# Softmax denominators in four column groups, one addition per quad, and unread products in every step

## What is computed

```
hi = x[src] @ w1
hj = x[tgt] @ w2
e = leaky_relu(hi + hj, negative_slope=0.3) * a
logits = e.reshape(-1, 8, 16).sum(axis=-1)            # 8 heads
exp = exp(logits - segment_max(logits, tgt)[tgt])
attn = exp / segment_sum(exp, tgt)[tgt]
out = segment_sum(hi.reshape(-1, 8, 16) * attn[:, :, None], tgt)
x = layernorm(x + out)
```

## Time and profile before

| | us |
|---|---|
| median of 3 runs | 2206.56 |
| lowest and highest run | 2199.6 and 2210.35 |
| the profiled execution, its own time | 2204.6 |
| its span in the trace | 2202.5 |

### The profile page before, as it was taken

One profiled execution on the slowest core, in us unless ns is written; L12 is line 12 of the kernel. 1 busy time (PEld: TensorE's weight loads), 2 busy tenths in 40 slices (PEclk: granted clock), 3 DMA queues, 4 the chain that ended last, 5 costly groups with the idle time before them and its releaser, 6 DMA issues.

```text
span 2202.5 us, 47203 instructions
## 1 busy us (share of the span) xinstructions
PE 1800.7 (82%) x12728; PEld 1400.5 (64%) x12729; DVE 1327.6 (60%) x3726; ACT 658.6 (30%) x1410; POOL 1605.9 (73%) x1701
## 2 busy tenths in 40 slices
PE   6678777988788788788969878888888888888886
PEld 6456555666566566566757666666766676666665
DVE  6455665666656666566645456666566566665665
ACT  6111211211111111111114434444444344434442
POOL 5777777777777777777627777777777777777774
PEclk8798998889988998889889999999999999999897
DMA  8722332323323333233255444444444444444441
GB/s 220 159 85 78 89 96 83 96 85 96 95 84 95 96 88 96 85 96 97 60 142 154 138 126 141 127 140 129 141 126 140 129 141 127 132 137 139 129 126 42
DMA packets 239386, 252.31 MB, mean 115 GB/s; under 512 B 141011, under 2 KB 187720, under 8 KB 239315
## 3 DMA queue, kind: packets, MB, share of 16 engines
q1 hardware_dynamic: 185036, 141.15, 21.5%
q0 software_dynamic: 54000, 110.28, 18.0%
q10 hardware_dynamic: 288, 0.13, 0.0%
HBM read 233.20 MB, written 13.22 MB: 112 GB/s over the span
## 4 chain that ended last, share of the span: by engine, by line
POOL 48%; issue 21%; PE 14%; DVE 7%; DMA 4%; DVEq 2%; POOLq 1%; ACT 1%; SPq 0%; ACTq 0%
POOL T L742 27%; POOL G L708 20%; PE ps L1847 2%; PE ps L1824 2%; DMA G<-hi_rows,idx 2%; PE ps L1819 2%; PE ps L1851 1%; DMA T<-y_rows,idx 1%; PE ps L1780 1%; PE ps L2061 1%; PE ps L2052 1%; DVEq L1309 1%; DVE msg L1329 1%; PE ps L2067 1%; PE ps L2073 1%
## 5 line engine op out<-in xcount | busy, mean ns | idle before, releaser
L742 POOL DMA_INDIRECT T<-y_rows,idx x831 | 789.0, 950 | 303.7 <-issue 249.2
L708 POOL DMA_INDIRECT G<-hi_rows,idx x831 | 801.9, 965 | 267.8 <-issue 249.0
L2052 PE MATMUL ps<-G 128*128 128x64 f32 x1664 | 228.5, 284 | 126.8 <-DVE acc L1606 126.2
L2052 PEld LDWEIGHTS ps<-G 128*128 128x128 f32 x1664 | 217.0, 204 | 138.7 <-issue 137.4
L993 ACT ACTIVATE G<-G 128x512 f32<-128x512 f32 x208 | 131.1, 630 | 576.6 <-DVE G L1612 576.6
L1819 PE MATMUL ps<-ident,G 128*128 128x128 f32 x828 | 151.0, 312 | 174.9 <-issue 60.0
L2061 PE MATMUL ps<-wN,G 128*128 128x128 f32 x1664 | 255.7, 302 | 26.3 <-DVE T L1571 26.0
L1612 DVE TENSOR_TENSOR G<-ps,T 128x512 f32<-128x512 f32 x208 | 143.6, 691 | 217.0 <-DMA T<-y_rows,idx 202.3
L890 ACT ACTIVATE V<-ps 128x512 f32<-128x512 f32 x207 | 123.6, 597 | 474.3 <-PE ps L1824 472.3
L1300 DVE TENSOR_TENSOR V<-ps,V 128x512 f32<-128x512 f32 x207 | 141.9, 686 | 179.5 <-ACT V L890 175.5
L2073 PEld LDWEIGHTS ps<-msg,wE 128*128 128x128 f32 x832 | 168.5, 203 | 125.2 <-issue 111.0
(11 more groups left out here) (233 smaller groups left out, 2252.3 us busy)
## 6 DMA issues: line engine op xcount, KB each, us to landing
T<-in_edge_weight SPq DMA_DIRECT2D x103, 512.0 KB
Dbc<-block_destinations SPq DMA_DIRECT2D x69, 384.0 KB
T<-in_edge_attr SPq DMA_DIRECT2D x103, 256.0 KB
G<-hi_rows,idx POOLq DMA_INDIRECT x831
T<-y_rows,idx POOLq DMA_INDIRECT x831, 2.5
link<-scan_destinations SPq DMA_DIRECT2D x280, 16.1 KB
hi_rows<-T SPq DMA_DIRECT2D x12, 256.0 KB, 2.8
mX<-in_x SPq DMA_DIRECT2D x15, 192.0 KB
```

The source lines that it names most:

```text
L708: pool.indirect_dma_start(out=G[:, s, t * C:(t + 1) * C], out_offset=None, in_=hi_d[:, :], in_offset=bass.IndirectOffsetOnAxis(ap=idx[:, s ...
L742: pool.indirect_dma_start(out=Yb[:, r, t * C:(t + 1) * C], out_offset=None, in_=y_d[:, :], in_offset=bass.IndirectOffsetOnAxis(ap=idx[:, r ...
L2052: ins = pe.matmul(aggP[:, 0:W], hS[i][:, n * C:(n + 1) * C], ohB[i][:, n * W:(n + 1) * W], start=(n == 0), stop=(n == 3))
```

## The change

1. `EXs` gets 32 columns per tile (9 used, the rest set to zero once). Each of a quad's four denominator products writes its own group of 32 output partitions, without accumulation across the four. The same in `sum_up`.
2. DVE adds both halves in one instruction per quad, [128, 2, 64]. Half 1 of the accumulator therefore has 128 live partitions, four partial sums of the denominators.
3. Where nodes are read back, PE no longer turns 9 partitions but multiplies the 128 partitions by `gather4`, a [128, 9] matrix with four ones per column that adds the four partial sums; `mD` has 128 partitions.
4. The DMA that clears half 1 covers 128 partitions.
5. `unread`: two products of `ident` with `W12` (256 columns) at the head of each step into `U[0]`, behind the wait for the previous maximum, and two ahead of a step's first aggregate into `AG[0]`.

```diff
-        EXs = sb("EXs", [P, GT, DC])
+        EXs = sb("EXs", [P, GT, 32])
+        gather4 = sb("gather4", [P, DC])
-        mD = sb("mD", [DC, MB * P])
+        mD = sb("mD", [P, MB * P])
+        accD4 = acc[:, 1, :]
...
-                        sp.dma_start(acc[0:DC, 1, :], acc[0:DC, 0, :]).then_inc(s_zero, 16)
+                        sp.dma_start(acc[:, 1, :], acc[:, 0, :]).then_inc(s_zero, 16)
...
-                        act.activation(mD[:, :], accD[:, cut], ACT.Copy).then_inc(s_n["copy"], 1)
+                        act.activation(mD[:, :], accD4[:, cut], ACT.Copy).then_inc(s_n["copy"], 1)
...
+            dve.memset(EXs[:, :, DC:32], 0.0)
+            dve.tensor_reduce(gather4[:, :], ident[:, :].rearrange("p (k h) -> p h k", k=4)[:, 0:DC, :], AX.X, ALU.add)
...
-                        w_ = acc[:, 0, bass.ds(base, W)]
-                        dve.tensor_tensor(w_, AG[j % 2][:, 0:W], w_, ALU.add).then_inc(s_acc, 1)
-                        w_ = accD[:, bass.ds(base, W)]
-                        dve.tensor_tensor(w_, AG[j % 2][0:DC, W:2 * W], w_, ALU.add).then_inc(s_acc, 1)
+                        w_ = acc[:, :, bass.ds(base, W)]
+                        dve.tensor_tensor(w_, AG[j % 2][:, 0:2 * W].rearrange("p (k n) -> p k n", k=2), w_, ALU.add
+                                          ).then_inc(s_acc, 2)
...
+                dve.memset(exsO[:, :, DC:32], 0.0)
                 dve.memset(exsO[:, :, 0:1], 1.0).then_inc(s_n["one"], 1)
...
+                    def unread(n, bank):
+                        for i in range(n):
+                            pe.matmul(bank[:, 0:2 * C], ident[:, :], W12[:, :], start=True, stop=True)
...
                         if j == 0:
+                            need(pe, s_acc, 2 * p * GQ)
+                            unread(2, AG[0])
                             pe.wait_ge(s_oh, p + 1)
...
-                            ins = pe.matmul(AG[j % 2][0:DC, W:2 * W], EXs[:, t, :],
-                                            oh[:, t * W:(t + 1) * W], start=(i == 0), stop=(i == 3))
+                            ins = pe.matmul(AG[j % 2][32 * i:32 * i + 32, W:2 * W], EXs[:, t, :],
+                                            oh[:, t * W:(t + 1) * W], start=True, stop=True, skip_group_check=True)
...
+                    if nq:
+                        need(pe, s_lk, (f - 1) * GQ + 1)
+                        unread(2, U[0])
                     sums(0, b, bs, 2)
...
-                            ins = pe.transpose(AG[1][:, MB * C + i * DC:MB * C + (i + 1) * DC], mD[:, i * P:(i + 1) * P],
-                                               ident[0:DC, 0:DC])
+                            ins = pe.matmul(AG[1][:, MB * C + i * DC:MB * C + (i + 1) * DC], mD[:, i * P:(i + 1) * P],
+                                            gather4[:, :], start=True, stop=True, skip_group_check=True)
```

More of the change, by code:

```diff
@@ L768, in build @@
         atP, h1P, efP, zP, aggP, oP = ps[0], ps[1:3], ps[3:5], ps[5:7], ps[7], ps[5]
-        exsO = R1[:, 0:4 * DC].rearrange("p (t h) -> p t h", h=DC)
+        exsO = R1[:, :].rearrange("p (t h) -> p t h", h=32)
         ohO = ohT[:, 1, :].bitcast(F32)
@@ L1923, in sum_up @@
                         t = 4 * j + i
-                        ins = pe.matmul(AG[j % 2][0:DC, W:2 * W], ex[:, t, :], hot[:, t * W:(t + 1) * W],
-                                        start=(i == 0), stop=(i == 3))
+                        ins = pe.matmul(AG[j % 2][32 * i:32 * i + 32, W:2 * W], ex[:, t, :], hot[:, t * W:(t + 1) * W],
+                                        start=True, stop=True, skip_group_check=True)
                     ins.then_inc(s_agg, 1)
@@ L1995, in _ @@
                     pe.transpose(ps[0][:, i * C:(i + 1) * C], accH[:, n0:n0 + P], ident[:, :])
-                    ins = pe.transpose(ps[3][:, i * DC:(i + 1) * DC], accD[:, n0:n0 + P], ident[0:DC, 0:DC])
+                    ins = pe.matmul(ps[3][:, i * DC:(i + 1) * DC], accD4[:, n0:n0 + P], gather4[:, :], start=True, stop=True,
+                                    skip_group_check=True)
                 ins.then_inc(s_n["t"], 1)
```

## The result

| | us |
|---|---|
| before, median (19 runs) | 2205.89 |
| changed, median (19 runs) | 2212.51 |
| ratio | 1.0027, 95% interval 1.0019 to 1.0035 |
| span of the profiled execution, before and after | 2202.5 and 2208.8 |

The kernel became 6.6 us slower. I had said 2221, so the sign is right and the size is less than half of what I forecast. A trace is that of one execution; its time can lie some us off the median of its kernel.

A forecast was written before the change was run, and what follows sets the result against it. POOL's gathers were taken to pace the softmax part, with no slack before the first reuse of a G slot. Copy 15, head products 1.6 and end -1.0 gave +15.6 us, so 2221 us, range 2208 to 2236.

The forecast's parts named there:

- The place: First reuse of a G slot: POOL waits for messages, and whatever delays the Dbc load's landing delays everything behind.
- The landing below 92 us: Sign at the Dbc load of group 2: expected to land about 98 us; below 92, the copy was over-priced.
- The term of 15 us: Clearing copy ahead of the Dbc load on SP's queue: 3.05 MB more, costing 15 us, with ends 12.3 and 19.8.
- no row here reaches that rate: Clearing copy: no shown row reaches the skill's 436 GB/s, by which the added delay would be 7 us, not 15.
- cheap copy: Rival at the clearing copy: it costs 6.1 us, result about 2212, or 2206 if wholly hidden; chance 0.18.
- Head products, +1.6 us: Two unread products on PE at the head of step 2, ahead of the messages, add 1.6 us to the chain.
- All other steps, 0: Remaining softmax steps: PE gains +0.9 us net per step, hidden by 2.6 us of room, so 0 us.
- the granted clock should stay up: PE through the softmax steps: less idle waiting keeps its clock up; the time saved is spent waiting, 0 us.
- fewer stretched gathers: Rival at POOL's gathers: L1379 never meets a gather's start, giving back 17.4 us, about 2203; chance 0.06.
- Small costs: Per quad of a step: one merged DVE addition takes 290 ns, the denominator sums on PE 0.27 us.
- The end, -1.0 us: From the last gather to the stored y rows: cheaper sums and additions less added products, -1.0 us (-1 to +1).
- the likeliest case: Whole kernel, forecast as priced: 2209 to 2232 us, from the copy's ends, gathers 5 us and runs 4 us either way; chance 0.64.

The follow-up runs named there:

- e1b: The changed kernel with the copy that clears accumulator half 1 issued behind the loads of group 2: 2205.06 us, ratio 0.9994 to the kernel before.
- e2b: The kernel before with only the clearing copy enlarged from 9 to 128 partitions, in its old place: 2211.99 us, ratio 1.0024.
- e11: The changed kernel with half of the clearing copy's columns ahead of the Dbc load, half behind the loads of group 2: 2206.54 us, ratio 1.0003.
- e4b: The changed kernel without the unread products inside the steps, clearing copy still ahead of the load: 2213.31 us, ratio 1.0034.
- e7: The changed kernel without unread products inside the steps and with the clearing copy behind the loads of group 2: 2209.35 us, ratio 1.0010.
- e12: The kernel before with both pairs of unread products added in each step and nothing else: 2210.61 us, ratio 1.0015.
- e14b: The changed kernel with the clearing copy behind the loads and DVE's 12-tile one-hot split into three instructions: 2195.67 us, ratio 0.9948.
- e16: The kernel before with only DVE's 12-tile one-hot split into three instructions: 2199.82 us, ratio 0.9971.
- e4: The changed kernel without unread products inside the steps, run on a slow chip: ratio 0.990 to the kernel before there.
- e14: The changed kernel with the clearing copy behind the loads and the one-hot in three instructions, on a slow chip: ratio 1.000.

## Why the prediction was right and wrong

**The place was right.** POOL paces the softmax part; the loss stands at the first reuse of a slot of `G`; it comes of the clearing copy ahead of the `Dbc` load. e1b takes it away, e2b makes most of it, and with half of the copy behind the loads, in e11, the landing is 3.6 us earlier and the loss is gone. The landing below 92 us, the sign that I had named for an over-priced copy, is what came.

**The term of 15 us was the mistake.** Measured it is 5.1 us (e2b alone), 5.3 (e4b against e7) and 7.3 us (changed against e1b), and the landing moved by 5.9. I had divided the added bytes by the rates that the DMA engines showed before, 154 to 248 GB/s. Those were the rates of other work: of the 6577 packets of that stretch 5643 were under 2 KB. That stretch had no long rows to compare with except nine of this same copy, and the engines moved the new copy's long rows far faster. The stretch that holds the landing in the changed kernel (rates in 40 slices of 74 to 86 us):

```profile
GB/s 195 744 104 40 229 293 561 256 181 241 439 457 385 283 625 256 270 423 710 198 297 710 341 270 410 724 198 297 352 386 167 447 263 338 406 297 297 326 388 282
...
DMA packets 873, 4.23 MB, mean 352 GB/s; under 512 B 210, under 2 KB 460, under 8 KB 756
```

Added bytes over added time is 3.05 MB in 5.9 us, 517 GB/s; between e11 and the full copy it is 457.

The trace of the kernel before did hold such a rate, outside the stretch that I had divided by. From 2 to 10 us, while `x` is loaded (rates in 40 slices, packets, issue):

```profile
GB/s 215 161 0 74 399 369 369 422 407 438 358 453 379 387 376 366 499 394 412 448 376 430 376 466 394 468 379 423 422 381 384 394 423 374 389 223 246 195 305 258
DMA packets 1160, 2.85 MB, mean 356 GB/s; under 512 B 155, under 2 KB 411, under 8 KB 1160
...
T<-in_x SPq DMA_DIRECT2D x4, 448.0 KB, 7.3
```

Two thirds of the packets have 2 KB or more there, and the rate is about 400 GB/s for 6 us. At 400 GB/s the added bytes take an estimated 7.6 us. So "no row here reaches that rate", in the prediction, is true of the rows that it shows and not of the trace.

The rival "cheap copy" had 6.1 us and 2212 in all; it came true in size and place. The Trainium skill's rule that I cited (DMA: Bandwidth & Descriptors, section Anatomy of one DMA) gave 7 us more for the new copy than for the old, by its 436 GB/s. The Trainium skill's page states this fit for transfers that GpSimd issues, and this copy is SyncE's; the trace is near it, with 5.9 us. I gave the rival 0.18 because the engines looked full and the old load had taken 13.88 us to land. A rate of short rows was no evidence against long ones.

**Head products, +1.6 us: wrong by their side effect.** They did take their time on the chain of step 2, 2.08 us with the first turns close behind. But logits and sums behind them ran faster, 0.65 and 0.82 us instead of 1.08 and 1.46 before, since the granted clock had risen by then. These are stretches of before (88 to 94 us) and after (94 to 97 and 97 to 104), in the columns explained above:

```profile
88.00:94.00 6.00, 5.26 (x35) 3.00 (x35) 2.00 (x4) 1.58 (x4) 4.72 (x5) 0.65 0.37 109
```

```profile
94.00:97.00 3.00, 2.85 (x8) 2.06 (x8) 0.96 (x2) 0.31 (x1) 1.47 (x2) 0.50 0.23 59
97.00:104.00 7.00, 6.59 (x61) 4.65 (x60) 4.38 (x7) 2.05 (x5) 1.22 (x2) 0.99 0.19 64
```

From the one-hot to the messages there are 10.53 us against 10.19 before, +0.3. In the kernel before, e12, both pairs of products together cost 3.3 us; its trace has that in the gathers and not at the head.

**All other steps, 0: right in the pace, wrong in two reasons.** The room of PE held: POOL's twelve waits for messages behind the first reuse make 3.7 us together. Not so "the granted clock should stay up": with the column groups it was lower, and the products only brought it back. And where DVE's instructions fell against the gathers changed, for 3 us in the traces, which the medians do not show by themselves. I had this as a rival with a gain ("fewer stretched gathers"); it went the other way. The Trainium skill's rule beside it (SBUF — State Buffer, section SBUF: two separate sides), that such instructions of VectorE and GpSimd exclude each other for a whole instruction, is what e14b and e16 bear out: shorter instructions, shorter meetings.

**Small costs.** The merged addition took 292 ns (predicted 290), a quad's denominators 0.25 to 0.29 us where the clock is full (0.27). On the chain at the end:

```profile
1099.96 0.86 PE ps L1841 x4
1100.83 0.84 PE ps L1857 x8
1101.66 0.25 PE ps L1861 x8
...
1133.98 0.16 PE ps L2008
1134.14 0.12 PE ps L2009 x2
```

**The end, -1.0 us: not seen.** From the last gather to the first `y` gather it is 51.4 us against 51.5. The parts came as worked out or better (a tile of the last nodes took 0.42 us before and 0.28 now, where I had added 0.15), and yet the piece ranges over 50.7 to 55.8 us across the twelve traces. A sum to a tenth of a us was finer than this piece repeats.

**The sum.** With the landing's 5.9 in place of 15 and 0.3 in place of 1.6, my working gives 5.9 + 0.3 - 1.0 = 5.2 us, and with 3 us of gathers 8; measured were 6.6. The range from 2208 held the result, and so did the likeliest case's own, from 2209, but by luck: its lower end was made of a copy of 12.3 us, with 5 us less of stretched gathers and 4 us for the spread of the runs. The copy took half of that, and the gathers became longer and not shorter.

## What to carry to other kernels

A bulk transfer that only has to be done "some time" belongs behind the loads that the next step waits for; look at what stands ahead of the first latency-critical load on each queue. Price added bytes by the rate of transfers with rows of the same length, not by the average of a busy stretch. Where gathers pace a kernel, look at the tail of their durations and at what VectorE was doing at their start: one two-input instruction of 0.95 us split in three won as much in the kernel before, 6.6 us, as the whole change lost.

## What the runs showed of the chip that I had not expected

- Four products of 32 columns into four groups of output partitions, in place of four accumulated ones of 9 columns, came with a granted clock of 0.77 over a whole stretch instead of 0.89 (e4b against before); shape and lighter work are not separated. Two pairs of unread products in each step raised it by 0.06 to 0.10.
- The same copy behind the same queue was priced at 154 to 248 GB/s from a stretch in which the DMA engines were busy throughout, and went at some 450 to 520. A busy DMA engine with short rows is no measure of what it moves with long ones.
- Splitting a VectorE instruction of 948 ns into three of 419 ns made GpSimd's gathers 11.9 us shorter over 831 of them, though VectorE worked longer.
- Two of the seven series ran on chips where the same program takes 1.5 times as long, with standstills of 9 to 10 us in PE once a step; the cause is open. On such a chip e4 had the ratio 0.990 where the same kernel has 1.0034 elsewhere, and e14 had 1.0004 where it has 0.9948.
